# An audio tower with attention and experts: order of the last jobs of a batch, and an early load of the gelu table

## The chip, the cores and the metric

One core of a Trainium2 chip runs the whole program. The metric is device time in microseconds (us), from the first to the last instruction with what lies around them; the kernel before took 1769.97 us, the median of three runs (1768.28 to 1775.53). The engines are TensorE (PE, with its weight loads shown apart as PEld), VectorE (DVE), ScalarE (ACT), GpSimd (POOL) and SyncE (SP, which issues DMAs). Each runs its own instructions in order and waits on semaphores for the others.

## The reference, cut to what matters

```python
def _block(x, cw, cb, gw, gb, stride):            # six times
    y = conv(x, cw, stride) + cb
    yg = y.reshape(B, 32, 4 * T)                  # 32 groups of 4 channels
    yn = (yg - yg.mean(-1)) * rsqrt(yg.var(-1) + 1e-5)
    return gelu(yn * gw + gb)                     # the tanh form

h = tower(x)                                      # 6 blocks, then a projection to 192
h = h + attention(layernorm(h))                   # 12 heads of 64, causal
xt = layernorm(h)
expert = argmax(softmax(xt @ gate_w + gate_b))    # the gate: 8 experts
h = h + ffn_of(expert)(xt)                        # exact gelu inside
```

The batch has 4 waveforms of 120000 samples. Two pieces of this meet in the change: the gate of the batch that ends, and the statistics of layer 0 of the batch that follows. The latter need no convolution: the mean and variance of a convolution's output follow from the sums of products of its input, so the kernel has scale and bias of the group norm before it computes layer 0.

## The kernel before, in words

The batches run in a loop, written out for every engine. In a batch the PE does a fixed list of jobs, and each job fills one of four slots of PSUM (a slot is 1024 float32 wide). For each phase (the convolution tower, six pairs of heads, and POST, the end of the batch) a list `JOBS` names the jobs, and who reads the result: DVE, ACT or both. The lists are in the order of the PE's instructions, and DVE and ACT walk the same lists, each doing the part of the jobs that is its own. Readers raise `act_freed` and `dve_freed`; the PE raises `ps_full` after each job.

`post_jobs` (L129 to L139) is the list of POST: "wo" (the attention's output projection, two jobs), "xt" (two jobs: transposes of the next batch's samples), "gram" (sums of products of the samples), "tr" (two jobs: transposes of the normalised tokens, one read by DVE, one by ACT), "taps" (the sums moved to filter taps), "chan" (mean and mean square of every channel of layer 0), "gate" (the logits of the 8 experts, 12 float32 matmuls, L1830 and L1831), and "group" (averages over the 4 channels of a group, one float32 matmul, L1597). Behind them stand two "pad" jobs, which make the number of jobs a multiple of four: a transpose on PE (L1833) and a copy of one column on DVE (L1430).

What DVE does for these at the end: for "chan", six small operations, the last of which writes `ms` (L1290); for "gate", two additions from PSUM (L1412, L1414) and seven small ones that make the one-hot choice (L1418 to L1427); for "group", `group_affine`: a copy of the averages (L1105), three small operations, a wait for POOL's power of -1/2 (L771), and three more, the last of which writes `affine` (L1120), the scale and bias of the group norm of layer 0. ACT has one job in POST, the copy of the second "tr" (L1014).

The next batch begins with the "conv0" jobs, two matmuls each (L1743). Before the first of them the PE waits until ACT and DVE have read everything of the batch before, pads included (`slot_free`, the case `n == 0`). ACT waits for `affine` and for the stores of the batch before, then for the first conv0 job, and writes `gelu(scale * x + bias)` (L987) into one of four buffers; DVE then splits each buffer into two float16 parts (L1207, L1209). ACT's functions come in table sets; the compiler puts an ACT_TABLE_LOAD ahead of an activation whose function isn't in the set that is sure to be loaded. Copy and Identity need none of their own. The batch uses two such functions: the tanh form of gelu in the tower, and Exp in the attention. The experts after the last batch use the exact gelu, which is a third (L1020).

After the last batch the PE ranks the tokens (L1842, L1843) once DVE and ACT are done and POOL has made its constants (L819 to L834, after POOL's last work of POST and the last PE job of it). DVE computes the slots (L1443 to L1463), and POOL scatters the tokens (L841).

Of the kernel before, what the change touches and what calls it, by code (L numbers as in the profile page):

```python
# [50 lines left out]
ACT_ENGINE, DVE_ENGINE = "act", "dve"  # L51
# [6 lines left out]
def tile_rows(i):  # L58
    return LASTM if i == TT - 1 else 128
# [67 lines left out]
def samples_jobs():  # L127

    return [("xt", (0,), (DVE_ENGINE,)), ("xt", (1,), (DVE_ENGINE,)), ("gram", (), (DVE_ENGINE,)),  # L129
            ("taps", (), (DVE_ENGINE,)), ("chan", (), (DVE_ENGINE,)), ("group", (0,), (DVE_ENGINE,))]  # L130


def post_jobs():
    jobs = [("wo", (0,), (DVE_ENGINE,)), ("wo", (1,), (DVE_ENGINE,))]

    xt0, xt1, gram, taps, chan, group = samples_jobs()
    jobs += [xt0, xt1, gram, ("tr", (0,), (DVE_ENGINE,)), ("tr", (1,), (ACT_ENGINE,)), taps,
             chan, ("gate", (), (DVE_ENGINE,)), group]
    return jobs  # L139


def setup_jobs():
# [5 lines left out]
SETUP, TOWER, PAIR, LAST_PAIR, POST, MOE = range(6)  # L148
JOBS = {SETUP: setup_jobs(), TOWER: tower_jobs(), PAIR: pair_jobs(False), LAST_PAIR: pair_jobs(True),
        POST: post_jobs()}  # L150


# [160 lines left out]
def audio_tower(nc, ins, out):  # L313
    fp32, fp16, bf16, i32 = mybir.dt.float32, mybir.dt.float16, mybir.dt.bfloat16, mybir.dt.int32
    ALU, ACT, AX = mybir.AluOpType, mybir.ActivationFunctionType, mybir.AxisListType
# [6 lines left out]
    with ctx:  # L322
        def sb(name, shape, dt=fp32):
            return ctx.enter_context(nc.sbuf_tensor(name, shape, dt))
# [19 lines left out]
        ones_col = sb("ones_col", [128, 1])  # L344
# [25 lines left out]
        spare = sb("spare", [128, 32])  # L370
# [121 lines left out]
        def slot(n):  # L492
            return ps[:, (n % 4) * 1024:(n % 4 + 1) * 1024]

        def bank(n, i):
            return ps[:, (n % 4) * 1024 + 512 * i:(n % 4) * 1024 + 512 * i + 512]
# [28 lines left out]
        def wait(eng, name, phase, k, b=None, pr=None):  # L525
            assert at(name, phase, k, 0, 0) > 0, (name, phase, k)
            eng.wait_ge(S[name], at(name, phase, k, b, pr))
# [338 lines left out]
        def _(act):  # L866
            a = nc.scalar

            def jobs_of(phase):
                for n in ACT_ORDER[phase]:  # L870
                    kind, args, who = JOBS[phase][n]
                    yield slot_of(phase, n), n, kind, args
# [13 lines left out]
            def normalise(layer, b):  # L886

                wait(act, "affine_ready", TOWER, layer, b)
                r = 0
                for rows in NORM_CHUNKS[layer]:  # L890
                    src = ys[layer][:, r * PITCH:(r + rows) * PITCH]
                    dst = src
                    if layer == 5:
                        all_rows = src.rearrange("p (r c) -> p r c", c=PITCH)
                        tokens = h5t.rearrange("p (c r) -> p r c", r=rows)
                        a.activation(tokens[:, :, 0:EARLY_COLS], all_rows[:, :, 0:EARLY_COLS],
                                     ACT.Gelu_apprx_tanh, bias=affine[:, 1:2], scale=affine[:, 0:1]
                                     ).then_inc(S["norm_done"], 1)
                        src, dst = all_rows[:, :, EARLY_COLS:COLS], tokens[:, :, EARLY_COLS:COLS]
                    a.activation(dst, src, ACT.Gelu_apprx_tanh, bias=affine[:, 1:2], scale=affine[:, 0:1]  # L900
                                 ).then_inc(S["norm_done"], 1)
                    r += rows
# [57 lines left out]
            with act.Fori(0, BATCH) as b:  # L960
                layer = 0
                for g, n, kind, args in jobs_of(TOWER):
                    if kind == "conv":
                        if args[0] > 1 and args[1] == 0:
                            normalise(args[0] - 1, b)
                        layer, r, cut = args
                        wait(act, "ps_full", TOWER, n + 1, b)
                        rows = cut[0]
                        dst = ys[layer][:, r * PITCH:(r + sum(cut)) * PITCH]
                        src = slot(g).rearrange("p (k n) -> p k n", k=2)[:, 0:len(cut), 0:rows * PITCH]  # L970
                        a.activation(dst.rearrange("p (k n) -> p k n", k=len(cut)), src, ACT.Identity,  # L971
                                     scale=1.0 / WSCALE).then_inc(S["act_freed"], 1)
                    elif kind == "conv0":
                        j, i = args
                        if args == (0, 0):
                            wait(act, "affine_ready", TOWER, 0, b)

                            wait(act, "scratch_stored", TOWER, 0, b)
                        wait(act, "ps_full", TOWER, n + 1, b)
                        piece = 3 * j + i  # L980
                        if piece >= STAGES:

                            had_it = (0, piece - STAGES)
                            wait(act, "hi_done", TOWER, SPLITS.index(had_it) + 1, b)
                            wait(act, "lo_done", TOWER, SPLITS.index(had_it) + 1, b)
                        src = slot(g).rearrange("p (m n) -> p m n", m=2)[:, :, 0:4 * PITCH]
                        a.activation(stage[:, piece % STAGES, :].rearrange("p (m n) -> p m n", m=2), src,  # L987
                                     ACT.Gelu_apprx_tanh,
                                     bias=affine[:, 1:2], scale=affine[:, 0:1]).then_inc(S["act_freed"], 1)
                    elif kind in ("q", "k", "v", "s"):  # L990
                        attention_job(TOWER, g, n, kind, args, b)
                    else:
                        assert kind == "xtr"
                        if layer == 5:
                            normalise(5, b)
                            layer = None
                            for p in range(LN_PARTS):
                                wait(act, "ln_scaled", TOWER, p + 1, b)
                                for i in (2 * p, 2 * p + 1):
                                    m = tile_rows(i)  # L1000
                                    last = a.activation(xn_hi[0:m, i, :], h[0:m, i, :], ACT.Identity,
                                                        bias=lnb[0:m, i:i + 1], scale=lnr[0:m, i:i + 1])
                                last.then_inc(S["xn_high"], 1)
                        wait(act, "ps_full", TOWER, n + 1, b)
                        a.activation(xt_parts[:, args[0], :], bank(g, 0).bitcast(fp16)[:, 0:TOK], ACT.Copy
                                     ).then_inc(S["act_freed"], 1)
                with act.Fori(0, PAIRS - 1) as pr:
                    for g, n, kind, args in jobs_of(PAIR):
                        attention_job(PAIR, g, n, kind, args, b, pr)
                for g, n, kind, args in jobs_of(LAST_PAIR):  # L1010
                    attention_job(LAST_PAIR, g, n, kind, args, b)
                for g, n, kind, args in jobs_of(POST):
                    wait(act, "ps_full", POST, n + 1, b)
                    a.activation(xnt1[0:D1, 0:TOK], slot(g)[0:D1, 0:TOK], ACT.Copy).then_inc(S["act_freed"], 1)  # L1014


            def take_hidden(j, par):
# [918 lines left out]
```

## Time and profile before

| | before |
|---|---|
| median of 3 runs | 1769.97 us (1768.28 to 1775.53) |
| the profiled execution's own time | 1773.54 us |
| its span, first to last instruction | 1771.9 us |
| PE busy | 1511.8 us, 85% |
| DVE busy | 1036.8 us, 59% |
| ACT busy | 766.5 us, 43% |
| POOL busy | 352.0 us, 20% |
| mean granted PE clock | 0.929 of 2.4 GHz |
| ACT_TABLE_LOADs | 24, 1.283 us each |

Times in the trace are us from the span's start. A row of the timeline has the start, the length, the engine, the line of the kernel, what it writes and reads with shapes, and how many instructions were merged into it; in brackets stands how long the engine was idle before, and who ended that.

### The profile page before, as it was taken

The page shows a single profiled execution, that of the slowest core. Times are in us where ns is not written, and L with a number is a line of the kernel's source. Part 1 is how long each engine was busy: PE and PEld are TensorE (multiplying, and loading weights), DVE is VectorE, ACT ScalarE, POOL GpSimd, SP SyncE. Part 2 cuts the span into 40 slices and gives each one's busy share as a digit, 9 for nine tenths or more (in the row PEclk, how much of TensorE's full clock was granted, in tenths as well). Part 3 has the DMA queues.
Part 4 walks back from the last instruction along what each step waited for, and adds up shares of the span by engine and source line. Part 5 has one row for each costly group of instructions (what it writes and reads, how often), then busy time and mean ns, then how long its engine had stood idle before and what let it go on. Part 6 is the DMA issues. An engine that isn't in the chain of part 4 may idle for free.

```text
span 1771.9 us, 32877 instructions
## 1 busy us (share of the span) xinstructions
PE 1511.8 (85%) x10257; PEld 1027.4 (58%) x10258; DVE 1036.8 (59%) x2386; ACT 766.5 (43%) x1484; POOL 352.0 (20%) x398
## 2 busy tenths in 40 slices
PE   5987799998976999989868999898779999059997
PEld 4433577783433777854436777643357778047775
DVE  5987555558885455578974555598745555212221
ACT  2654455526643555345635555265445552012231
POOL 2000234300002334100003432000023430612111
PEclk9998899998988999989888999899889999579999
DMA  4300122210001222110002221100024423611110
GB/s 107 114 1 1 36 61 48 57 37 12 1 1 26 45 61 48 32 39 1 1 1 62 48 57 45 39 1 1 1 72 97 119 59 106 188 49 49 47 51 17
DMA packets 105852, 81.31 MB, mean 46 GB/s; under 512 B 57842, under 2 KB 96267, under 8 KB 105747
## 3 DMA queue, kind: packets, MB, share of 16 engines
q1 hardware_dynamic: 99988, 70.65, 15.9%
q0 software_dynamic: 5760, 9.36, 1.8%
q8 instruction: 54, 0.88, 0.2%
q14 instruction: 50, 0.41, 0.1%
HBM read 34.66 MB, written 18.38 MB: 30 GB/s over the span
## 4 chain that ended last, share of the span: by engine, by line
issue 50%; PE 35%; POOL 4%; DVE 4%; ACT 2%; DMA 2%; SPq 1%; DVEq 0%; POOLq 0%; ACTq 0%
PE ps L1721 9%; PE ps L1663 4%; PE ps L1695 4%; PE ps L1881 4%; PE ps L1707 4%; PE ps L1861 3%; PE ps L1862 2%; PE ps L1670 2%; DVE arena L1236 2%; POOL slot_scratch L841 1%; PE ps L1869 1%; SPq L550 1%; ACT arena L955 1%; PE ps L1882 1%; DMA slot_scratch<-arena 1%
## 5 line engine op out<-in xcount | busy, mean ns | idle before, releaser
L1770 PE MATMUL ps<-arena,cwt 128*128 128x504 f16 (+2 forms) x1776 | 389.4, 379 | 37.0 <-DVE arena L1207 32.6
L1770 PEld LDWEIGHTS ps<-arena,cwt 128*128 128x128 f16 x1776 | 172.8, 101 | 253.9 <-DVE arena L1207 52.9
L1228 DVE TENSOR_REDUCE nmax<-ps 128x1 f32<-128x128 f32 (+5 forms) x288 | 177.1, 615 | 177.7 <-PE ps L1698 177.6
L1721 PE MATMUL ps<-arena 128*128 128x64 f32 (+2 forms) x2016 | 260.1, 269 | 9.3 <-DVE arena L1236 5.1
L1721 PEld LDWEIGHTS ps<-arena 128*128 128x128 f32 (+2 forms) x2016 | 241.8, 189 | 26.1 <-issue 17.9
L1209 DVE TENSOR_TENSOR arena<-arena 128x1008 f16<-128x1008 f32 (+4 forms) x200 | 227.1, 1135 | 6.9
L1236 DVE COPY arena<-ps 128x512 f32<-128x512 f32 (+4 forms) x288 | 156.3, 543 | 85.0 <-PE ps L1707 79.7
L914 ACT ACTIVATE arena<-ps,nmax 128x128 f32<-128x128 f32 (+5 forms) x288 | 180.9, 628 | 38.7 <-DVE nmax L1228 38.3
L1695 PE MATMUL ps<-arena 128*128 128x512 f16 (+6 forms) x780 | 163.6, 313 | 29.0 <-ACT arena L955 16.3
L1707 PE MATMUL ps<-ident,arena 128*128 128x128 f32 (+2 forms) x1008 | 165.1, 281 | 10.6 <-ACT arena L955 5.7
L971 ACT ACTIVATE arena<-ps 128x1008 f32<-128x1008 f32 (+1 forms) x112 | 96.0, 866 | 176.7 <-PE ps L1770 176.7
L955 ACT ACTIVATE arena<-ps,rinv 128x64 f32<-128x64 f32 (+1 forms) x288 | 91.0, 316 | 149.7 <-PE ps L1721 146.6
L1207 DVE CAST arena<-arena 128x1008 f16<-128x1008 f32 (+4 forms) x200 | 128.3, 641 | 27.6 <-ACT arena L900 16.1
L900 ACT ACTIVATE arena<-arena,affine 128x1008 f32<-128x1008 f32 (+5 forms) x108 | 111.2, 1107 | 76.5 <-DVE affine L1120 76.5
L1707 PEld LDWEIGHTS ps<-ident,arena 128*128 128x128 f32 (+2 forms) x1008 | 109.5, 144 | 49.1 <-ACT arena L955 38.4
L771 POOL TENSOR_TENSOR tmp<-tmp,neg_half 128x1 f32<-128x1 f32 x25 | 13.9, 555 | 622.4 <-DVE tmp L1110 622.4
L1340 DVE BATCH_NORM_STATS2 bn<-arena 128x6 f32<-128x500 f32 (+1 forms) x180 | 103.0, 630 | 16.7 <-ACT arena L971 16.7
L1695 PEld LDWEIGHTS ps<-arena 128*128 128x128 f16 (+2 forms) x780 | 77.4, 118 | 59.8 <-ACT arena L955 21.7
L1020 ACT ACTIVATE arena<-ps 128x768 f32<-128x768 f32 x31 | 25.2, 813 | 195.4 <-PE ps L1862 195.4
L987 ACT ACTIVATE arena<-ps,affine 128x1008 f32<-128x1008 f32 x96 | 107.0, 1193 | 0.2
L780 POOL TENSOR_TENSOR arena<-arena,ones_col 128x750 f16<-128x750 f32 x40 | 57.4, 1435 | 183.7 <-ACT arena L932 183.7
L1543 PE MATMUL ps<-cwt,ident_h 128*128 128x512 f16 x248 | 75.8, 447 | 0.0
(255 smaller groups left out, 2170.6 us busy)
## 6 DMA issues: line engine op xcount, KB each, us to landing
arena<-arena SPq DMA_DIRECT2D x96, 187.5 KB, 2.9
arena<-arena SPq DMA_DIRECT2D x96, 93.8 KB, 2.3
slot_scratch<-empty_slot SPq DMA_DIRECT2D x1, 5775.0 KB, 19.0
arena<-in_L_ffn_w SPq DMA_DIRECT2D x8, 576.0 KB
arena<-in_L_ffn_w SPq DMA_DIRECT2D x8, 384.0 KB
arena<-slot_scratch SPq DMA_DIRECT2D x31, 96.5 KB, 1.9
arena<-slot_scratch SPq DMA_DIRECT2D x31, 96.0 KB, 2.0
xa<-in_x POOLq DMA_DIRECT2D x5, 468.8 KB, 4.4
```

Of the source, the lines that this page charges most:

```text
L900: a.activation(dst, src, ACT.Gelu_apprx_tanh, bias=affine[:, 1:2], scale=affine[:, 0:1]).then_inc(S["norm_done"], 1)
L914: a.activation(prob[k % PROBS][0:m, 0:128 * i + m], slot(g)[0:m, 0:128 * i + m], ACT.Exp, bias=nmax[0:m, k_:k_ + 1], accum_out=rsum[0:m, k ...
L955: a.activation(z[0:m, i, DH * hh:DH * hh + DH], slot(g)[0:m, Z_AT:Z_AT + DH], ACT.Copy, scale=rinv[0:m, k:k + 1]).then_inc(S["act_freed"], 1)
L987: a.activation(stage[:, piece % STAGES, :].rearrange("p (m n) -> p m n", m=2), src, ACT.Gelu_apprx_tanh, bias=affine[:, 1:2], scale=affine ...
L1207: v.tensor_copy(high, src).then_inc(S["hi_done"], 1)
L1209: v.tensor_tensor(low, src, high, ALU.subtract).then_inc(S["lo_done"], 1)
L1228: v.reduce_max(nmax[0:m, k_:k_ + 1], slot(g)[0:m, 0:128 * i + m], AX.X, negate=True).then_inc(S["smax_done"], 1)
L1236: v.tensor_copy(probt[k % 2][:, 0:w, 0:m], src[:, 0:w, 0:m]).then_inc(S["dve_freed"], 1)
L1695: last = t.matmul(slot(g)[0:m, lo:hi], q, keys[:, lo:hi], start=a == 0, stop=a == len(terms) - 1 and not diagonal)
L1707: last = t.transpose(slot(g)[0:kk, 128 * c:128 * c + m], prob[k % PROBS][0:m, 128 * c:128 * c + kk], ident[0:m, 0:m])
L1721: last = t.matmul(slot(g)[0:m, Z_AT:Z_AT + DH], probt[k % 2][0:kk, c, 0:m], vt[0:kk, c, DH * hh:DH * hh + DH], start=c == 0, stop=c == i)
L1770: last = t.matmul(bank(g, k)[:, 0:c * PITCH].rearrange("p (r c) -> p r c", c=PITCH), cwt[layer][:, w, tap, :], parts[x][:, f:f + 2 * c - 1 ...
```

## The change

"group" moves ahead of "gate" in the list of POST, so the PE and the DVE both do it first. And at the end of POST, behind its one copy, ACT runs a gelu (tanh form) on one column into a spare column that nothing reads.

```diff
@@ post_jobs
     jobs += [xt0, xt1, gram, ("tr", (0,), (DVE_ENGINE,)), ("tr", (1,), (ACT_ENGINE,)), taps,
-             chan, ("gate", (), (DVE_ENGINE,)), group]
+             chan, group, ("gate", (), (DVE_ENGINE,))]
     return jobs
@@ the ACT program, end of a batch
                 for g, n, kind, args in jobs_of(POST):
                     wait(act, "ps_full", POST, n + 1, b)
                     a.activation(xnt1[0:D1, 0:TOK], slot(g)[0:D1, 0:TOK], ACT.Copy).then_inc(S["act_freed"], 1)
+
+                a.activation(spare[:, 30:31], ones_col[:, :], ACT.Gelu_apprx_tanh)
```

## Rows read from the trace of the kernel before

**Rows 1.** The page, engines: busy time, share of the span, instructions.
```profile
PE 1511.8 (85%) x10257; PEld 1027.4 (58%) x10258; DVE 1036.8 (59%) x2386; ACT 766.5 (43%) x1484; POOL 352.0 (20%) x398
```

**Rows 2.** Timeline of DVE, end of the first batch and start of the second.
```profile
395.34 0.16 DVE L1290 SCALAR_TENSOR_TENSOR ms<-mv,tmp 128x1 f32<-128x1 f32 x1
399.99 0.20 DVE L1412 TENSOR_TENSOR logits<-ps,gate_b 128x40 f32<-128x40 f32 x1 [4.49 <-PE ps L1831]
...
402.08 0.16 DVE L1105 COPY gm<-ps 128x2 f32<-128x2 f32 x1
...
403.61 0.21 DVE L1120 SCALAR_TENSOR_TENSOR affine<-tmp,channel_par 128x1 f32<-128x1 f32 x1
403.74 0.22 DVE L1430 COPY spare<-ps 128x1 f32<-128x1 f32 x2
406.82 0.69 DVE L1207 CAST arena<-arena 128x1008 f16<-128x1008 f32 x1 [2.87 <-ACT arena L987]
```

**Rows 3.** Timeline of PE, the same stretch.
```profile
394.34 0.38 PE L1830 MATMUL ps<-gw,arena 128*128 128x8 f32 x2
...
395.29 0.59 PE L1831 MATMUL ps<-gw,arena 64*128 64x8 f32 x2
395.81 0.59 PE L1830 MATMUL ps<-gw,arena 128*128 128x8 f32 x2
...
399.88 0.59 PE L1597 MATMUL ps<-ms,group_avg 128*128 128x2 f32 x2
404.01 5.12 PE L1743 MATMUL ps<-xt,cw0t 105*128 105x504 f16 x12 [3.02 <-DVE spare L1430]
```

**Rows 4.** Timeline of ACT, the same stretch.
```profile
392.26 0.79 ACT L1014 ACTIVATE arena<-ps 64x750 f32<-64x750 f32 x1 [21.54 <-PE ps L1636]
404.01 1.28 ACT L987 ACT_TABLE_LOAD   x1 [10.96 <-DVE affine L1120]
405.31 6.61 ACT L987 ACTIVATE arena<-ps,affine 128x1008 f32<-128x1008 f32 x6
```

**Rows 5.** PE at the start of the first batch: averages, pads, conv0.
```profile
33.55 0.56 PE L1597 MATMUL ps<-ms,group_avg 128*128 128x2 f32 x2 [2.10 <-DVE ms L1290]
33.98 0.88 PE L1626 MATMUL ps<-ident 128*128 128x128 f32 x3
```

**Rows 6.** DVE and ACT there: averages' operand, their copy, table load, first gelu.
```profile
33.25 0.16 DVE L1290 SCALAR_TENSOR_TENSOR ms<-mv,tmp 128x1 f32<-128x1 f32 x1
34.15 0.16 DVE L1105 COPY gm<-ps 128x2 f32<-128x2 f32 x1 [0.74 <-PE ps L1597]
...
36.71 1.28 ACT L987 ACT_TABLE_LOAD   x1 [1.64 <-DVE affine L1120]
```

**Rows 7.** ACT_TABLE_LOADs by line: busy us, mean ns | idle before them.
```profile
L1020 ACT ACT_TABLE_LOAD x15 | 19.2, 1283 | 0.3
...
L987 ACT ACT_TABLE_LOAD x4 | 5.1, 1283 | 34.5 <-DVE affine L1120 34.5
```

**Rows 8.** Line L1743, PE, 404 to 405.4: ns min/median/max.
```profile
L1743 PE MATMUL ps<-xt,cw0t x4: 602/627/627, 404.0 to 405.2; 105*128 105x504 f16 x4
```

**Rows 9.** Stages: length, engines' busy us (count), PEclk, DMA share, GB/s.
```profile
412.00:416.00 4.00, 4.00 (x13) 1.45 (x11) 3.93 (x5) 0.00 (x0) 0.00 (x0) 0.57 0.00 0
416.00:432.00 16.00, 16.00 (x77) 6.98 (x75) 15.76 (x22) 10.46 (x11) 0.00 (x0) 1.00 0.00 0
```

**Rows 10.** End of the last batch: DVE, then POOL, then PE.
```profile
1512.52 0.36 DVE L1443 COPY arena<-ps 128x192 f32<-128x192 f32 x1 [2.29 <-POOL arena L834]
...
1509.54 0.20 POOL L819 MEMSET arena<- 128x128 f32 x1
...
1506.61 0.67 PE L1833 MATMUL ps<-ident 128*128 128x128 f32 x2
1510.52 0.98 PE L1842 MATMUL ps<-onehot,arena 128*128 128x192 f32 x2 [3.25 <-POOL arena L821]
1511.29 0.85 PE L1843 MATMUL ps<-onehot,arena 128*128 128x192 f32 x2
```

## The prediction

> **What bounds the kernel now.** The change touches the end of a batch, so I read the page first, then the timelines there. On the page the PE is busy 85% of the span, DVE 59%, ACT 43% [rows 1]: taken over all, PE binds. But shares don't decide here; at the end of a batch no engine is full. The timelines of DVE, PE and ACT, side by side, show who waits for whom [rows 2 to 4]. DVE finishes the channel statistics `ms` at 395.50 and is then idle for 4.49 us, until the PE's gate matmuls end [rows 2]. It does the gate's choice, then the averages' chain from 402.08 on, then two pad copies, up to 403.96. Only then may the PE start conv0, at 404.01; it had been idle 3.02 us and names the pad copy L1430 as what it waited for [rows 3]. ACT was idle 10.96 us and waited for `affine`; it loads the gelu table at 404.01 (1.28 us) and runs the first gelu at 405.31 [rows 4]. DVE's first split follows at 406.82 [rows 2], and from 416 on DVE and PE are both nearly full (15.76 and 16.00 of 16 us) [rows 9]. The path is therefore: PE gate, DVE gate choice, DVE averages' chain, pads, then ACT's table load beside the first conv0 job, and ACT's gelu.
>
> **The averages leave the end of DVE's list.** Before, their chain is 402.08 to 403.74, 1.66 us, on the path [rows 2]. After, it lies in DVE's idle time. `ms` comes at 395.50. At the start of the first batch, where the PE does wait for `ms` as it will now, `ms` ended at 33.41, the matmul started at 33.55 and the copy L1105 at 34.15, so 0.14 us to the matmul and 0.74 us to the copy [rows 5, 6]. So the copy starts at 396.24, and 1.66 us later, near 397.9, `affine` is written. The cover is the wait for the gate, which lasts until about 402; without it the 1.66 us would be back on the path.
>
> **The gate leaves the place where it was hidden.** This is the price. The gate's matmuls start at 394.34 now, right behind "chan", while DVE is still computing `ms` [rows 3]. After, the averages' matmul stands ahead of them in the PE's queue and waits for `ms`, and the 24 gate matmuls, both pads and the next conv0 are queued behind that wait. The matmul starts at 395.50 + 0.14 = 395.64, and the next one follows 0.43 us behind it (33.55 to 33.98 [rows 5]): the gate starts at 396.07, 1.73 us late.
>
> It will also be slower. Before, three of its twelve pairs start 0.32 us apart, and from 395.29 on they are 0.52 us apart [rows 3]: the granted clock fell from 2.4 to 1.2 GHz after the last of the sample work, while the gate ran. After, all twelve are behind that fall: 3 x (0.52 - 0.32) = 0.60 us more. The gate took 399.88 - 394.34 = 5.54 us, and will take 6.14 us; it ends at 402.21 instead of 399.88, 2.33 us late. The two bounds are: the clock falls as late behind the gate's start as it does now, so that the gate keeps 5.54 us (1.73 us late); and the clock stays up for the whole gate, 12 x 0.32 = 3.8 us, so that it ends at 399.9, as before (0.0 late). I take the first value, 2.33, because the wait put in gives the PE less to do ahead of the gate, not more.
>
> The Trainium skill speaks against the change here. "TensorE: Matmul & The Clock Gate", Part 1, says that the PE's clock depends on how busy it has been, and that half rate is the default after idleness. The trace agrees as far as it goes: 1.2 GHz from 395.29 on and until conv0. By this rule the gate would be wholly at 1.2 GHz, which is the value taken from the rows.
>
> **Sum on the path to conv0.** Gate 2.33 us later, averages' chain 1.66 us shorter: conv0 starts 0.67 us later, at 404.68. DVE's other work in between (gate choice, pads) stays as it is. The PE's pads follow the gate and are done before DVE gets to them.
>
> **The touch of the gelu table.** After L1014, at 393.05, ACT has nothing to do until `affine` [rows 4], so the added activation and the load ahead of it (1.28 us and about 0.2) cost nothing. Is the load at L987 gone, then? I think not. The loop's first pass comes from the setup with another set (the load at 36.71 [rows 6]), so at the loop's head no set is sure. The experts' loop shows what the compiler does in such a case: L1020 is the only line there that needs a set, each pass ends with it loaded, and the loads are 15, one for each pass [rows 7]. So I expect 8 loads of the tanh set instead of 4. It matters little. The load at L987 stands behind the wait for `affine` and ahead of that for conv0's result, and `affine` now comes near 397.9. The load runs there, hidden, with or without the touch: the reorder takes it off the path, not the touch.
>
> What that is worth: conv0 starts at 404.01, its second matmul 0.41 us later ((5.12 - 0.63) / 11 [rows 3, 8]), and that takes 0.63 us, to 405.05; with about 0.05 us for the handing over (DVE's gate work started 0.04 us after the last gate matmul ended) ACT could have begun at 405.10. It began at 405.31. So the load cost about 0.20 us, not 1.28. "ScalarE: Activation LUTs" of the Trainium skill, What ACT_TABLE_LOAD costs, gives 2.66 us for a switch of sets, of which about 1.38 us is a drain. Here the activation starts 1.30 us after its load does [rows 4]; with 2.66 us it would have started at 406.67, and hiding the load would be worth 1.56 us for each batch.
>
> **The sum.** For each start of a batch behind another: +0.67 - 0.20 = +0.47 us at the first gelu, and from there the whole shifts, since DVE goes on at its own pace from its first split. There are three such starts. The first batch has its averages from the setup, whose list isn't touched; its load at 36.71 stays. 3 x 0.47 = +1.4 us.
>
> **The last batch.** Behind it comes the ranking. DVE starts L1443 at 1512.52, when both the PE's second matmul (1511.29 + 0.85 = 1512.14, and some handing over) and POOL's last constant are there; the rows name POOL, which began its constants at 1509.54, after its power for the averages [rows 10]. After, POOL's power is done early, and POOL waits for the PE's last pad instead: it ended at 1507.28, and goes to about 1507.28 + 2.33 - 0.43 (the averages' matmul no longer follows the gate [rows 5]) = 1509.2. That is 0.3 to 0.4 us earlier for POOL. The matmuls of the ranking started at 1510.52, when a constant of POOL's came, and they also need DVE's last step, which comes 0.67 us later than now; at the most they move to 1511.2. I put this at +0.2 us, between -0.4 (POOL decides) and +0.67 (PE decides).
>
> Total: +1.6 us. The profiled execution had a span of 1771.9 us and a time of 1773.54 us, which would become 1773.5 and 1775.1. The median of the runs is 3.6 us below the profiled time; the same sum on it gives 1771.6 us.
>
> **Rivals.**
> 1. The gate keeps the full clock. Then it ends as before, and the path is 1.66 us shorter: conv0 at 402.4, ACT's gelu -1.66 - 0.20 = -1.86 us, three times -5.6, with the last batch -6.0: 1764.0 us. For it: the fall comes about 0.95 us behind the gate's start, which is close, and what decides it is not in a row. Against it: it must hold for 6 us more, with an idle PE in between. A lesser form of it is the first bound (5.54 us): +0.07 - 0.20 each, -0.4 in all, 1769.6.
> 2. Slower: the clock stays low for longer in the new batch. From 416 on the PE is busy for all of the 16 us at full clock, and it has nothing to give; from 412 to 416 it runs at a mean of 0.57 while DVE is still the one that is full (3.93 of 4) [rows 9]. With the PE's work about 0.5 us later for each batch passed, the next rise may come late. Three more microseconds at half clock there cost 1.5 us of the PE's work; it decides as soon as the PE's backlog is beyond DVE's. Price 3 x 1.5 = 4.5 us on top: 1776.1 us. Against it: conv0 itself is long and dense both before and after.
> 3. The load at L987 is really gone, because the compiler takes the touch at the loop's end as sure. It would be gone in the first batch too, and the setup would have to provide it. Its worth is 1.28 us once, and none in the others: +0.3, 1770.3 us. Against: the 15 loads [rows 7].
> 4. The early `affine` lets conv0 begin early, as the order suggests: it would be so if conv0 waited for `affine` alone. Then conv0 would follow the PE's last pad, near 403.1, 0.9 us earlier, and the sum is -3.3 us, 1766.7. Against: the PE names the DVE pad copy [rows 3], and the pads come behind the gate in DVE's list too.
>
> **How the numbers follow.** Forecast (+1.6) 0.65, its lesser form (-0.4) 0.08, full clock (-6.0) 0.06, late rise (+6) 0.12, load gone (+0.3) 0.05, conv0 early (-3.3) 0.02, something else 0.02. All lie inside 0.5% (8.8 us), about what a measurement of this kernel can tell from no change. The runs of before span 7.3 us by themselves, so a median may stray by 3. The range goes from 1765.5 (the lesser form less the stray, short of the full clock) to 1777.0 (late rise and a little stray). Faster 0.02, same 0.94, slower 0.04.
>
> **What would show it.** Right: DVE's idle time ahead of L1412 is split in two, with L1105 to L1120 between 396.2 and 398; the gate's pairs all 0.52 us apart, and its last near 402.2 less the start; PE idle some 1.2 us behind "chan"; conv0 still waiting for L1430, near 404.7; the load at L987 near 398 and four more loads on the new line; ACT's first gelu now waiting for the PE, near 405.8. Wrong: gate pairs at 0.32 us (rival 1); a mean granted clock well below 0.929 and PE waits gone in the tower (rival 2); four loads of the tanh set instead of eight (rival 3). If the first gelu starts where I say and the time differs by more than a few us, the cause lies outside the end of the batch, and the sum was made in the wrong place.

## The result, and the profile after

The changed kernel took 1778.89 us (median of 11 runs, 1774.35 to 1785.72), the kernel before 1773.12 us in the same comparison (11 runs, 1765.62 to 1775.53). The ratio is 1.0039, with a 95% interval of 1.0023 to 1.0055: about 7 us slower (4 to 10). That is inside 0.5%, but clear of no change, and beyond the upper end of the range (1777.0). Some 3 of the 7.3 us between the forecast and the measured median lie in the base: the three runs of before that the forecast stood on had a median of 1769.97.

Page of the changed kernel, engines:
```profile
PE 1511.2 (85%) x10257; PEld 1026.0 (58%) x10258; DVE 1038.5 (58%) x2386; ACT 772.5 (44%) x1492; POOL 351.5 (20%) x398
```
No share has moved by more than a point [rows 1]; ACT has its eight new instructions. The span is 1775.3 us, 3.4 more than before, with a mean granted clock of 0.919 instead of 0.929.

Timeline of DVE, changed kernel, end of the first batch and start of the second (answers to rows 2):
```profile
394.64 0.16 DVE L1292 SCALAR_TENSOR_TENSOR ms<-mv,tmp 128x1 f32<-128x1 f32 x1
395.27 0.16 DVE L1107 COPY gm<-ps 128x2 f32<-128x2 f32 x1 [0.48 <-PE ps L1599]
...
396.81 0.21 DVE L1122 SCALAR_TENSOR_TENSOR affine<-tmp,channel_par 128x1 f32<-128x1 f32 x1
400.12 0.20 DVE L1414 TENSOR_TENSOR logits<-ps,gate_b 128x40 f32<-128x40 f32 x1 [3.10 <-PE ps L1833]
...
402.22 0.26 DVE L1432 COPY spare<-ps 128x1 f32<-128x1 f32 x2
407.06 0.68 DVE L1209 CAST arena<-arena 128x1008 f16<-128x1008 f32 x1 [4.57 <-ACT arena L987]
```
PE, the same stretch (rows 3):
```profile
393.30 0.39 PE L1595 MATMUL ps<-tap_sums,cw0f 10*128 10x11 f32 x2 [0.31 <-DVE tap_sums L1276]
394.85 0.38 PE L1599 MATMUL ps<-ms,group_avg 128*128 128x2 f32 x2 [1.17 <-DVE ms L1292]
395.10 0.37 PE L1832 MATMUL ps<-gw,arena 128*128 128x8 f32 x2
...
396.99 0.59 PE L1832 MATMUL ps<-gw,arena 128*128 128x8 f32 x2
...
400.01 0.69 PE L1835 MATMUL ps<-ident 128*128 128x128 f32 x2
402.55 4.98 PE L1745 MATMUL ps<-xt,cw0t 105*128 105x504 f16 x12 [1.84 <-DVE spare L1432]
411.48 6.05 PE L1772 MATMUL ps<-arena,cwt 128*128 128x504 f16 x14 [3.95 <-DVE arena L1209]
```
ACT, the same stretch (rows 4), and POOL:
```profile
392.37 1.28 ACT L1016 ACT_TABLE_LOAD   x1
393.66 0.20 ACT L1016 ACTIVATE spare<-ones_col 128x1 f32<-128x1 f32 x1
397.21 1.28 ACT L987 ACT_TABLE_LOAD   x1 [3.34 <-DVE affine L1122]
403.61 4.44 ACT L987 ACTIVATE arena<-ps,affine 128x1008 f32<-128x1008 f32 x4 [5.12 <-PE ps L1745]
```
```profile
401.52 0.61 POOL L749 DMA_DIRECT2D xa<-in_x  x1 [5.01 <-PE ps L1835]
```
Read them from the top. The averages' chain now lies in DVE's wait for the gate, the table load in ACT's wait for conv0, and conv0 starts 9.25 us behind "chan" (393.30 to 402.55) instead of 10.01: earlier, not later. ACT's first gelu comes 1.06 us behind it and ends near 404.80. And then the surprise: DVE's first split starts only at 407.06. The row names ACT as the releaser, but ACT had been done for 2.3 us. The time was lost there.

POOL shows what else had moved. In the kernel before it issued the load of the samples of the next batch at 404.01, behind its power for the averages:
```profile
402.76 0.56 POOL L771 TENSOR_TENSOR tmp<-tmp,neg_half 128x1 f32<-128x1 f32 x1 [14.58 <-DVE tmp L1110]
404.01 0.61 POOL L749 DMA_DIRECT2D xa<-in_x  x1 [0.69 <-issue]
```
Now that power is done early, POOL waits for the PE's last pad alone, and issues at 401.52. DVE, at the same time, comes to the end of its loop's body and has to go on at the body's head. The DMA view of the kernel before, from 404.80 to 405.25, just behind DVE's pads (first line: the window in 40 slices, busy tenths; then the queues):
```profile
DMA  0000090000000000000000000000000000000000
...
q14 instruction: 1, 0.01, 4.7%
```
One 8 KB packet of the instruction queue, at 404.86, ahead of the samples, whose first packet comes at 405.31. The changed kernel, 402.48 to 404.60 and then 404.60 to 405.30:
```profile
q0 software_dynamic: 68, 0.47, 84.4%
```
```profile
q0 software_dynamic: 44, 0.01, 11.8%
q14 instruction: 1, 0.01, 5.4%
```
The samples come first, from 402.83 on, and the instruction packet comes at 404.70: 2.2 us behind DVE's pads instead of 0.9. The view names the queue and not the engine, so that this packet carries DVE's code is my reading. What speaks for it: at all 39 boundaries (13 traces, three each) such a packet comes 0.9 to 2.9 us behind DVE's pads, and DVE's first split starts 1.9 to 2.4 us behind it.

### The profile page after: what moved, and what is told of

It reads as the page before. It is cut to its first block, busy times and chain, and to the rows that moved or that the text cites. A ratio compares the mean times of both kernels' runs of the same rounds, so it can differ in the third digit from the quotient of the medians.

```text
span 1775.3 us, 32885 instructions
## 1 busy us (share of the span) xinstructions
PE 1511.2 (85%) x10257; PEld 1026.0 (58%) x10258; DVE 1038.5 (58%) x2386; ACT 772.5 (44%) x1492; POOL 351.5 (20%) x398
## 4 chain that ended last, share of the span: by engine, by line
PE 47%; issue 38%; DVE 5%; POOL 3%; ACT 2%; DMA 2%; SPq 1%; DVEq 1%; POOLq 0%; ACTq 0%
PE ps L1723 12%; PE ps L1697 5%; PE ps L1709 5%; PE ps L1665 4%; PE ps L1883 4%; PE ps L1818 3%; PE ps L1863 3%; PE ps L1864 2%; DVE arena L1238 2%; PE ps L1672 2%; POOL slot_scratch L841 1%; ACT arena L955 1%; PE ps L1871 1%; SPq L550 1%; PE ps L1731 1%
## 5 line engine op out<-in xcount | busy, mean ns | idle before, releaser
L1772 PE MATMUL ps<-arena,cwt 128*128 128x504 f16 (+2 forms) x1776 | 396.9, 385 | 41.1 <-DVE arena L1209 38.7
L1772 PEld LDWEIGHTS ps<-arena,cwt 128*128 128x128 f16 x1776 | 176.7, 103 | 261.6 <-DVE arena L1209 57.7
L1709 PE MATMUL ps<-ident,arena 128*128 128x128 f32 (+2 forms) x1008 | 164.6, 281 | 10.7 <-ACT arena L955 5.7
L987 ACT ACTIVATE arena<-ps,affine 128x1008 f32<-128x1008 f32 x96 | 107.4, 1192 | 21.5 <-PE ps L1745 16.4
L1480 DVE COPY arena<-ps 128x512 f32<-128x512 f32 x31 | 21.2, 682 | 93.5 <-PE ps L1871 93.5
```

Source lines behind the costliest of these rows:

```text
L1709: last = t.transpose(slot(g)[0:kk, 128 * c:128 * c + m], prob[k % PROBS][0:m, 128 * c:128 * c + kk], ident[0:m, 0:m])
L1772: last = t.matmul(bank(g, k)[:, 0:c * PITCH].rearrange("p (r c) -> p r c", c=PITCH), cwt[layer][:, w, tap, :], parts[x][:, f:f + 2 * c - 1 ...
```

## The experiments

For each boundary between batches I read three numbers from the starts in the timelines: from "chan" to conv0, from conv0 to DVE's first split, and from the split to the end of the operation that writes `affine` of layer 1 (the last of its averages) in the batch that begins.

| kernel | "chan" to conv0 | conv0 to first split | layer 1 | ratio (95%) |
|---|---|---|---|---|
| before | 10.0, 10.0, 10.0 | 2.8, 2.8, 3.1 | 65.0, 65.0, 65.2 | 1 |
| changed | 9.3, 9.1, 10.7 | 4.5, 4.8, 4.2 | 66.2, 66.2, 65.8 | 1.0039 (1.0023 to 1.0055) |
| e1 reorder only | 10.7, 9.2, 9.2 | 4.2, 4.8, 4.5 | 66.0, 66.1, 65.0 | 1.0032 (1.0015 to 1.0049) |
| e2 touch only | 10.1, 10.1, 10.1 | 3.2, 2.8, 2.8 | 65.0, 65.2, 65.1 | 0.9996 (0.9984 to 1.0008) |
| e3 changed, samples late | 9.4, 9.3, 10.7 | 2.8, 2.8, 2.8 | 65.0, 65.0, 65.0 | 0.9985 (0.9969 to 1.0001) |
| e4 before, samples late | 10.1, 10.1, 10.1 | 3.1, 2.9, 2.8 | 65.0, 65.0, 65.0 | 0.9998 (0.9989 to 1.0008) |
| e5 changed, more to load | 10.7, 9.2, 10.7 | 4.3, 4.2, 4.4 | 66.0, 65.0, 65.9 | 1.0016 (1.0004 to 1.0027) |
| e6 changed, samples behind the pads | 9.3, 10.7, 9.4 | 2.8, 2.8, 2.8 | 65.0, 65.0, 65.0 | 0.9984 (0.9967 to 1.0001) |
| e7 gate split, samples late | 9.0, 8.9, 8.8 | 2.8, 3.1, 2.8 | 65.8, 65.9, 66.1 | 0.9985 (0.9973 to 0.9996) |
| e8 changed, filler | 10.7, 10.7, 10.7 | 4.3, 5.0, 3.8 | 65.0, 65.0, 65.0 | 1.0026 (1.0012 to 1.0039) |
| e9 gate split, late, filler | 8.9, 9.1, 8.8 | 3.1, 2.8, 3.1 | 65.0, 65.0, 65.0 | 0.9965 (0.9952 to 0.9978) |
| e10 before, filler | 10.2, 10.1, 8.4 | 2.8, 3.1, 2.8 | 65.0, 65.0, 65.0 | 0.9995 (0.9979 to 1.0011) |
| e11 changed, late, filler | 10.7, 10.7, 9.3 | 2.8, 2.8, 3.1 | 65.0, 65.0, 65.0 | 0.9997 (0.9985 to 1.0009) |

**e1 and e2: each half of the change alone.** e1 has only the new order of the list, e2 only the touch:
```diff
+                a.activation(spare[:, 30:31], ones_col[:, :], ACT.Gelu_apprx_tanh)
```


> Only the order of the list is changed; ACT doesn't touch the gelu table. Theory A (the sample load collides with DVE's code): the new order frees POOL earlier, so the load of the next samples starts near 1.4 us ahead of conv0 instead of beside it, and DVE's first split comes 13.7 to 14.9 us behind the start of 'chan' as in the changed kernel (12.8 to 13.1 before). Time about +4 to +6 us over the kernel before, like the changed kernel. Theory B (the added activation and its four table loads cost the time): distance 12.8 to 13.1 and time as before. Theory C (chance phase of the PE's clock, nothing else): the distance keeps its +1 us, and the time is anywhere within 3 us of before.

> Only the touch of the gelu table is added, the order of the list stays. Theory A: distance from 'chan' to DVE's first split 12.8 to 13.1 us, time within 1.5 us of before; 28 table loads instead of 24, the four new ones in ACT's idle time. Theory B: time +4 to +6 us. The load in front of the first gelu of a batch stays, at 1.28 us, in every batch.

The reorder alone brings a loss like the changed kernel's (the two intervals overlap for most of their length) and the same late split, 13.6 to 14.9 us behind "chan"; the touch alone brings neither. The loads by line in e2 (busy us, mean ns, idle before):
```profile
L1022 ACT ACT_TABLE_LOAD x15 | 19.2, 1283 | 0.2
L987 ACT ACT_TABLE_LOAD x4 | 5.1, 1283 | 30.2 <-DVE affine L1122 30.2
...
L1016 ACT ACT_TABLE_LOAD x4 | 5.1, 1283 | 0.1
```
Four loads more, and the four at L987 are still there. The touch loads a table that is loaded again before it is used.

**e3 and e4: the samples' load later, in either order.** In POOL's loop, ahead of the load:
```diff
                 wait(pool, "ps_full", TOWER, 0, b)
+                wait(pool, "act_freed", TOWER, 6, b)
```


> The changed kernel, in which POOL also waits until ACT has done its sixth conv0 piece before it starts the load of the next samples; so the load can't run while DVE comes round its loop. Theory A: DVE's first split comes about 12.0 us behind 'chan' (13.8 to 14.9 in the changed kernel), the PE's idle time between conv0 and the first convolution of layer 1 falls from 4.0 to about 2.3 us, and the low stretch of the clock there is no longer than before. Time: about 2 us below the kernel before, 5 to 8 below the changed one. Theory C or another cause for DVE's late start: distance 13.8 to 14.9 as in the changed kernel, time as the changed kernel's.

> The kernel before, with the same added wait of POOL ahead of the load of the samples. Theory A: in the kernel before DVE's code came just ahead of the samples (404.9 against 405.3), so the later load gives back 0.3 us for each batch at the most: distance 12.5 to 12.8, time within 1.5 us of before. If the wait itself did something else for the time (the load of samples in the tower costing or sparing something), this kernel would show it alone.

With the load out of the way, DVE's split starts 2.8 us behind conv0 in every batch, and the loss is gone: the interval ends at 1.0001, and the changed kernel's begins at 1.0023. In the old order the same wait changes nothing (12.8 to 13.2 us from "chan" to the split; the 0.3 us that it was to give back did not come). So the place of the load makes the loss, as theory A says. e3's timeline of POOL, DVE and the PE:
```profile
411.82 0.61 POOL L749 DMA_DIRECT2D xa<-in_x  x1 [14.89 <-ACT arena L988]
...
405.96 0.68 DVE L1210 CAST arena<-arena 128x1008 f16<-128x1008 f32 x1 [2.89 <-ACT arena L988]
...
410.38 1.93 PE L1773 MATMUL ps<-arena,cwt 128*128 128x504 f16 x5 [2.45 <-DVE arena L1210]
```
The distance from "chan" to the first split was 12.1 to 12.2 us in two batches, as expected, and 13.5 in the third. There the clock fell ahead of the gate, and "chan" to conv0 took 10.7 us. That spread comes with the samples early or late, so it isn't theirs. The gain over before, 2.7 us by the ratio (-0.2 to 5.5), is what the expectation said, but not clear of none.

**e5: more to load.** One more load ahead of the samples', of 560 columns into an unused tile:
```diff
                 wait(pool, "ps_full", TOWER, 0, b)
+                pool.dma_start(xdup[:, :], ins["x"][bass.ds(b, 1), :].rearrange("a (p n) -> (a p) n", n=PER_COL)[:, 0:560]
+                               ).then_inc(dup_loaded, 16)
                 load_samples((b + 1) & (BATCH - 1))
+                pool.wait_ge(dup_loaded, b * 16 + 16)
```

> The changed kernel, in which POOL puts one more load ahead of that of the samples: 560 of 960 columns of a waveform (0.28 MB on top of 0.48 MB), into a tile that nothing reads. If DVE's code waits behind the samples in the DMA engines (theory A), DVE's first split comes about 1.4 us later than in the changed kernel (58% more of a traffic that lasts 2.5 us), so 15.2 to 16.3 us behind 'chan', and the time rises by some 4 us over the changed kernel's. If DVE's late start has another cause (its own loop, ACT, a semaphore), the distance stays at 13.8 to 14.9 and the time at the changed kernel's.

The distance stays: 4.2 to 4.4 us from conv0 to the split, though the traffic now lasts 4 us; and the time is no longer than the changed kernel's, rather less. So the code doesn't wait until all of the traffic is through, and this part of theory A was wrong. In this kernel the code's packet comes 1.7 to 1.9 us behind the first data packet, in the changed one 1.6 to 2.2 us.

What it does wait for is open, because the added load stands ahead of the samples and pushes them back. POOL in e5:
```profile
404.86 0.61 POOL L794 DMA_DIRECT2D xdup<-in_x  x1 [6.10 <-PE ps L1840]
405.59 0.53 POOL L751 DMA_DIRECT2D xa<-in_x  x1
```
The DMA view of e5, from 405.90 to 410.40, and then only to 407.85, just ahead of the instruction packet at 407.91:
```profile
q0 software_dynamic: 192, 0.76, 65.1%
```
```profile
q0 software_dynamic: 103, 0.46, 85.4%
```
When the packet came, 0.46 MB had passed, and 0.47 MB in the changed kernel (first boundary of each). A wait for the part of the traffic that is queued ahead of the code isn't excluded by this run. "DMA: Bandwidth & Descriptors" of the Trainium skill, Queues, rings and completion order, says that each DMA engine goes round its queues one packet at a time, and that a packet can gather many descriptors. That would give a wait that doesn't grow with the amount; no row here shows the packets inside an engine.

**e6: only behind the pads.** The wait of e3 is replaced by one for DVE's pads.
```diff
+                wait(pool, "dve_freed", TOWER, 0, b)
```


> The changed kernel, in which POOL starts the load of the samples only when DVE has done its pads, as it was by itself before the change (404.01 against 403.96). If what matters is only which of the two comes first, the samples or DVE's code, this small delay of about 1 us is enough: the first packets of the samples come near 1.3 us behind conv0's start, DVE's code slips in ahead of them, and the distance is 12.0 to 12.6 us as with the late load. If the samples still overtake the code, the distance lies between 12.6 and 14.

```profile
405.37 0.61 POOL L749 DMA_DIRECT2D xa<-in_x  x1 [6.80 <-DVE spare L1433]
...
407.45 0.68 DVE L1210 CAST arena<-arena 128x1008 f16<-128x1008 f32 x1 [2.89 <-ACT arena L988]
```
The instruction packet came at 405.52, the samples' first at 406.69, and the split was as early as with the late load (2.8 us at all three boundaries; 12.1, 13.5 and 12.1 us from "chan", the middle one with the clock down ahead of the gate). So it is enough that the samples come behind the packet, if only by one microsecond.

**e7: split gate, late samples.** The PE runs three of the gate's six tiles ahead of the averages' matmul, while it would wait for `ms`:
```diff
+                    if kind == "group":
+                        slot_free(POST, n + 1, b)
+                        gate_matmuls(slot_of(POST, n + 1), range(3), b)
 ...
                     elif kind == "gate":
+                        last = gate_matmuls(g, range(3, TT), b)
```


> The changed kernel with the late load of the samples, and in the PE's program half of the gate's matmuls (the first three of six tiles) run ahead of the averages' matmul, in the 1.2 us in which it waits for ms. If the rest of the path is as I read it, the gate then ends about as early behind 'chan' as in the kernel before plus one matmul (6.1 us; 6.9 with the whole gate behind the averages in the run of the late load), and DVE's first split comes 11.3 to 11.6 us behind 'chan'. Time about 4 us below the kernel before, 0.9975. If DVE's loop head is now what binds, the distance doesn't fall below 12.

The path to the first split fell to 11.6 to 11.9 us, where 11.3 to 11.6 were expected, but layer 1 took 0.8 to 1.1 us longer, and the time was 0.9985 instead of 0.9975. The stages (length, busy us of the engines, granted clock) say why; first e7, then e9 with the filler, from its first conv0 on:
```profile
395.00:415.00 20.00, 16.15 (x48) 8.91 (x49) 12.34 (x32) 7.99 (x7) 1.69 (x3) 0.50 0.12 30
```
```profile
405.00:411.00 6.00, 5.98 (x15) 2.19 (x16) 2.80 (x4) 4.92 (x5) 0.00 (x0) 0.51 0.01 3
411.00:418.00 7.00, 5.97 (x28) 2.29 (x25) 6.90 (x8) 3.20 (x4) 1.14 (x2) 1.00 0.27 69
```
In e7 the PE is at 1.2 GHz all the way to 415.4, through the first convolutions of layer 1; the clock had not risen at all.

**e8 and e9: fillers.** Dense matmuls on the PE where it waits for DVE's first parts of layer 0 (8 in the changed kernel, 5 in e7's):
```diff
                         if layer > 1 and r == 0:
                             keep_busy(g, 6)
+                        if layer == 1 and r == 0:
+                            keep_busy(g, 8)          # e9, e10, e11: 5
```


> The changed kernel, in which the PE runs 8 filler matmuls of 512 columns behind its last early conv0 job (3.4 us at 1.2 GHz), where it is idle for 3.95 to 4.2 us before the first convolution of layer 1. Their result is overwritten. If the second part of the loss comes from the clock, which falls again because of that idle time (6.8 us at 1.2 GHz instead of 3.4), the stretch from DVE's first split to the averages of layer 1 returns from 66.0 to 66.2 us to 65.0 or below, while the distance from 'chan' to the first split stays at 13.8 to 14.9. Time 3 us below the changed kernel, 1.0022 of before. If the longer stretch had come from DVE or ACT, it stays at 66 and the fillers change nothing.

> The kernel with the split gate and the late load of the samples, with 5 filler matmuls at the same place (2.15 us at 1.2 GHz, for an idle time of 2.0 to 2.3 us). There the distance from 'chan' to the first split is 11.6 to 11.9 us, but layer 1 takes 65.8 to 66.0 us, since the clock stays at 1.2 GHz from the gate on for 20.5 us. If the clock is what takes the gain back, layer 1 returns to 65.0 and the time is 0.9970 to 0.9975 of before (5 us below). If it isn't, the time stays at 0.9985.

Layer 1 is back at 65.0 us in all six batches, as expected, while in e8 the late split stays at 3.8 to 5.0 us. There the clock fell ahead of the gate at all three boundaries (10.7 us), so that the distance from "chan" to the split was 14.5 to 15.6 us. In the time, e8's 1.0026 isn't clear of the changed kernel's 1.0039: the intervals overlap. e9 is faster than both kernels: 0.9965 (0.9952 to 0.9978), 6 us below the kernel before.

**e10 and e11: whose gain is it?** The fillers on the kernel before, and on e3.

> The kernel before, with 5 filler matmuls at the same place (idle time there 2.1 to 2.4 us). It separates the gain of the fillers from that of the split gate and the late load. Layer 1 took 65.0 to 65.2 us in the kernel before, with 3.4 us at 1.2 GHz; the fillers can't make it much shorter if DVE sets its pace then. Expected: distance from 'chan' to the first split 12.8 to 13.1, layer 1 65.0, time 0.999 to 1.000 of before. If the fillers alone give 0.997, the gain of the combined kernel is theirs.

> The changed kernel with the late load of the samples and 5 filler matmuls: the combined kernel without the split gate. Expected: distance 12.1 to 12.2 where the clock falls while the gate runs, 13.5 where it fell before; layer 1 65.0; time 0.998 of before. The combined kernel's further gain over this one is the split gate's.

The fillers alone give nothing, since layer 1 was at 65.0 before. e11 gives 0.9997 where 0.998 was expected; it had the clock fall ahead of the gate in two of three batches (10.7 us), and the interval of e3, the same kernel without fillers, overlaps its own. e9's interval lies wholly below e11's, so most of e9's gain goes with the split gate, which brings "chan" to conv0 to 8.8 to 9.1 us in every batch. That it needs the fillers too is what layer 1 says (65.8 to 66.1 us in e7, 65.0 in e9); the times (0.9985 and 0.9965) point the same way, but their intervals touch. That it needs the late samples as well is argued from e3, and was not tried in this kernel.

## Why the prediction was wrong, point by point

**The averages' chain.** Right. `affine` came 3.5 us behind "chan" (396.81 against 393.30) and hides in the wait for the gate, which still lasts 3.10 us. The matmul began 0.05 us behind `ms`, the copy 0.47 us, a little faster than the setup's.

**The gate.** The term was mis-sized at two of three boundaries. Forecast: all twelve pairs 0.52 us apart, conv0 0.67 us later. In two of three batches six of the pairs still ran 0.32 us apart (395.10 to 396.99): the granted clock fell later behind "chan" than before, 3.7 us instead of 1.3. The gate took 4.91 us instead of 5.54, and conv0 came 0.8 to 0.9 us earlier. In the third batch the clock fell before the gate, and conv0 came 0.65 us later, as forecast. The value taken, "the wait put in gives the PE less to do", assumed that the fall goes by the PE's work just then. In the runs that have the whole gate behind the averages it falls either way, from one batch to the next (9.1 to 9.4 or 10.7 us from "chan" to conv0). Nor is that the reorder's alone: in e10, which has the old order, one batch had 8.4 us where the others had 10.1 and 10.2. The prediction also let the low clock end at conv0; before the change it rose only at 408.6, in conv0's last microsecond.

**The table.** Right: eight loads instead of four; the one at L987 runs at 397.21, hidden. The touch starts 1.29 us after its load does (392.37 and 393.66), so the 1.38 us of drain that the Trainium skill has in "ScalarE: Activation LUTs" don't show here either. ACT began 1.06 us behind conv0, forecast 1.09.

**"From there the whole shifts, since DVE goes on at its own pace from its first split."** This is the step that failed. The first gelu, behind "chan", came 1.0 and 1.1 us earlier than before and in the third batch 0.4 us later (forecast: 0.47 later at all three); the first split did not shift with it, but came 0.9, 1.1 and 1.8 us later. From gelu to split it was 1.5, 1.5 and 1.8 us before and 3.5, 3.7 and 3.2 us after. I followed DVE's first split from ACT alone. DVE's own path was not looked at: its loop ends there, and the code at the loop's head, as I now read the traces, comes by DMA. Nor was POOL's queue followed at these three boundaries, though I did so at the last batch: its power for the averages moved ahead, so what stands behind it, the load of the samples, moved too, from beside conv0's start to 1 us ahead of it. In rows 2 the sign was there: DVE was idle 2.87 us and started at 406.82, while ACT's first piece had ended at 406.50, and hand-overs take 0.04 us. Measured, this costs 4.5 us from conv0 to the split instead of 2.9, 1.6 us for each boundary; e3 and e6 take it away, e1 has it without the touch. "Runtime: NRT & Kernel Launch" of the Trainium skill, Instruction fetch mechanics, says that a taken branch out of the current pages has to wait for a DMA fetch of its target. The traces agree as far as they go: where no samples are ahead, an instruction packet comes 0.9 to 1.2 us behind the pads, and DVE's first instruction 1.9 to 2.2 us behind the packet.

**The late rise of the clock** was rival 2, with a chance of 0.12. It happened at all three boundaries, but for a reason that I had not named. PE's conv0 comes early and DVE's split late, so that the PE is idle for 3.95 to 4.2 us between them (L1772 above) instead of 2.1 to 2.4. In the kernel before:
```profile
411.24 5.68 PE L1770 MATMUL ps<-arena,cwt 128*128 128x504 f16 x18 [2.11 <-DVE arena L1207]
```
The low stretch behind it lasts 6.8 us instead of 3.4. The two stretches, before and then changed:
```profile
412.10:415.50 3.40, 3.40 (x10) 1.23 (x9) 3.33 (x5) 0.00 (x0) 0.00 (x0) 0.53 0.00 0
```
```profile
410.50:417.40 6.90, 5.92 (x15) 2.11 (x16) 6.76 (x9) 1.19 (x1) 0.00 (x0) 0.51 0.00 0
```
Stage from 410 to 418, before and then changed, granted clock 0.79 and 0.57:
```profile
410.00:418.00 8.00, 6.76 (x24) 2.63 (x24) 7.86 (x11) 2.94 (x4) 0.00 (x0) 0.79 0.00 0
```
```profile
410.00:418.00 8.00, 6.53 (x17) 2.37 (x18) 7.86 (x9) 1.46 (x2) 0.00 (x0) 0.57 0.00 0
```
The price was 1.2, 1.2 and 0.6 us in layer 1, against 1.5 forecast, and e8 removes it. Where the stretch was short (3.4 us in e1's last batch) layer 1 took 65.0 us with a late split too (4.5 us): so it is the clock, not the split.

**The last batch.** "chan" to L1443 (L1445 in the changed kernel): 12.44 us before, 12.57 after; forecast +0.2. DVE's row names POOL before and the PE's second matmul after; the forecast had left open which of the two would decide.

**The sum.** From "chan" to the first split the three boundaries lost 0.94, 1.12 and 1.79 us, together 3.9; layer 1 another 3.0. That makes 6.8 us, and the ratio says 6.9. That the two meet is in part luck. The span of the one profiled execution grew by only 3.4 us, because its attention stages were shorter: from the first split to the next "chan" it took 1.2 us less in two batches although layer 1 was longer, and 0.8 more in the last. In the traces of the changed kernel and e1 this distance is 354.4 to 354.7 us in five of six batches, in those of before, e2 and e4 it is 355.5 to 355.9 in all nine, and within e3's trace it is 352.9, 355.5 and 352.9. How much of layer 1's 3.0 us reaches the time is therefore not shown: e3 and e6 take away the late split and the long stretch of low clock together, and e8, which takes away the second alone, isn't clear of the changed kernel. What is shown is that both together go with the place of the samples' load, and the loss with them.

**The range.** Its lower end doesn't follow from what it names: the lesser form less the stray is 1769.6 - 3 = 1766.6 us, not 1765.5. The result lies beyond the other end.

## What to carry to other kernels

When a step is moved, follow every queue that it leaves: an engine that is free sooner issues its next DMA sooner (here POOL, 1 us ahead of conv0 instead of beside it), and that DMA may delay another engine at its loop's end. A "waited for" row whose releaser had been done for more than a hand-over is a sign of something the row doesn't name; look at the instruction queue of the DMA view there. And where a producer gets faster and its consumer doesn't, the idle time between them can lower the PE's clock for the work behind it.

## What the runs showed of the hardware

- At its loop's end DVE starts again 2.8 to 3.2 us behind conv0's start (the pads end 0.05 us before that) where no samples are ahead: 0.9 to 1.2 us to an 8 KB packet of the instruction queue and 1.9 to 2.2 us more. Where a load from POOL has its first packets ahead of that packet, it is 3.8 to 5.0 us. With 0.28 MB put in ahead of that load (e5) it is 4.2 to 4.4 us, no longer than without.
- The granted clock, at 1.2 GHz since the gate, stayed there until 415.4 in e7, which has conv0 in between; in the first batch of the other kernels it rose at 407 to 411. With five dense matmuls in the idle time behind conv0 it was at 2.4 GHz through the first convolutions of layer 1 (PEclk 1.00 from 411 to 418 in e9).
- Four more table loads of 1.28 us in an idle stretch cost nothing that can be measured (0.9996, 0.9984 to 1.0008).
